# Differential attention in chunks of 384 queries, in five batches of 4, 4, 4, 3 and 3 key tiles

## The reference, cut to what matters

```python
Q, K, V = proj(q_w), proj(k_w), proj(v_w)      # (2, 8 heads, 2304 tokens, 64)
Q1, Q2 = Q[..., :32], Q[..., 32:]
K1, K2 = K[..., :32], K[..., 32:]
attn1 = softmax(Q1 @ K1^T * 32 ** -0.5)        # (2, 8, 2304, 2304)
attn2 = softmax(Q2 @ K2^T * 32 ** -0.5)
out = (attn1 - lam * attn2) @ V                # lam: one number per head
```

## Time and profile before

| what | value |
|---|---|
| time, median of 3 runs | 5568.89 us (5566.74 to 5574.1) |
| the profiled execution's own time | 5571.24 us |
| its span | 5569.4 us, 60834 instructions |
| PE, DVE, ACT, POOL busy over the span | 92%, 60%, 43%, 54% |
| differential attention: first pair to last normalised output | 245 to 3249 us |
| batch loop of it, first score to last value product's end | 282 to 3231 us |

### The profile page before, as it was taken

How to read it: one execution, slowest core, us unless ns; L and a number is a source line. 1 busy time by engine, 2 the same in 40 slices (tenths; PEclk the granted TensorE clock), 3 DMA queues, 4 the chain that set the end, 5 groups by cost and what they waited for, 6 DMA issues and landing times. The chain is left out here.

```text
span 5569.4 us, 60834 instructions
## 1 busy us (share of the span) xinstructions
PE 5106.0 (92%) x21620; PEld 2895.0 (52%) x21620; DVE 3339.3 (60%) x3947; ACT 2405.3 (43%) x4669; POOL 2985.2 (54%) x1379
## 2 busy tenths in 40 slices
PE   8799999999999999999999969879997898898699
PEld 4455545554555455545554424467774555555355
DVE  3466676677777767777677625465553445445484
ACT  3255555555555555555555522124442333333332
POOL 0088888888888888888888831046663000000000
PEclk9799999999999999999999978889998999999999
DMA  6611111111111111111111036442201000000101
GB/s 224 195 34 31 38 37 38 31 39 37 41 28 39 37 41 28 39 37 44 25 39 37 14 99 172 154 116 69 69 18 63 9 20 23 17 23 11 47 9 52
DMA packets 220119, 295.43 MB, mean 53 GB/s; under 512 B 77918, under 2 KB 186822, under 8 KB 212302
## 3 DMA queue, kind: packets, MB, share of 16 engines
q1 hardware_dynamic: 219856, 292.05, 18.6%
HBM read 178.11 MB, written 113.87 MB: 52 GB/s over the span
## 5 line engine op out<-in xcount | busy, mean ns | idle before, releaser
L658 POOL TENSOR_TENSOR diff_run_pool<-diff_run_pool,diff_probs 128x1024 f32<-128x1024 f32 (+1 forms) x960 | 2214.3, 2307 | 156.6 <-ACT diff_probs L505 19.6
L584 DVE TENSOR_REDUCE diff_maxes<-diff_max 128x1 f32<-128x768 f32 x1728 | 1539.2, 951 | 834.6 <-PE diff_max L425 833.4
L505 ACT ACTIVATE diff_probs<-diff_ring 128x512 f32<-128x512 f32 (+1 forms) x2880 | 1434.6, 558 | 1008.0 <-PE diff_ring L412 1002.2
L451 PE MATMUL diff_out_ps<-diff_probs,diff_vs 128*64 128x512 f32 (+1 forms) x5760 | 1222.4, 559 | 0.0
L425 PE MATMUL diff_max<-diff_ks,diff_qs 96*128 96x384 f32 x3456 | 977.0, 366 | 129.6 <-DVE diff_maxes L584 94.3
L412 PE MATMUL diff_ring<-diff_qs,diff_ks 97*128 97x512 f32 (+1 forms) x2880 | 1043.9, 397 | 3.3 <-ACT diff_probs L505 2.0
L425 PEld LDWEIGHTS diff_max<-diff_ks,diff_qs 96*128 96x128 f32 x3456 | 584.9, 191 | 472.9 <-DVE diff_maxes L584 392.6
L412 PEld LDWEIGHTS diff_ring<-diff_qs,diff_ks 97*128 97x128 f32 x2880 | 504.2, 188 | 388.0 <-issue 346.4
L451 PEld LDWEIGHTS diff_out_ps<-diff_probs,diff_vs 128*64 128x64 f32 x5760 | 371.8, 137 | 583.7 <-issue 441.7
L2041 POOL MEMSET ffn_before<- 128x128 f32 x1 | 0.2, 204 | 987.7 <-POOLq L63 987.7
L1373 POOL TENSOR_TENSOR causal_run_sum<-causal_run_sum,causal_probs 128x768 f32<-128x768 f32 (+2 forms) x208 | 340.7, 1638 | 74.7 <-ACT causal_probs L1247 52.7
(11 more groups left out here) (229 smaller groups left out, 5827.5 us busy)
## 6 DMA issues: line engine op xcount, KB each, us to landing
qk_hi<-proj_hi SPq DMA_DIRECT2D x12, 1536.0 KB, 5.8
qk_lo<-proj_lo SPq DMA_DIRECT2D x12, 1536.0 KB, 9.5
diff_qs<-qk_hi SPq DMA_DIRECT2D x64, 288.0 KB, 4.4
diff_ks<-qk_hi SPq DMA_DIRECT2D x64, 288.0 KB, 6.1
diff_recip<-row_factors SPq DMA_DIRECT2D x128, 128.0 KB, 2.8
o_rows<-diff_normed SPq DMA_DIRECT2D x64, 256.0 KB, 2.0
v_rows<-proj_vst SPq DMA_DIRECT2D x12, 768.0 KB, 7.6
diff_qs<-qk_lo SPq DMA_DIRECT2D x32, 288.0 KB, 5.3
```

Of the source, the lines that this page charges most:

```text
L451: mm = pe.matmul(out_ps[VD * j:VD * (j + 1), 0:w], vs[n % 2][:, g, j, :], probs[g % PBUF][:, j, 0:w], start=g == 0, stop=g == STEPS - 1, t ...
L505: act.activation(probs[g % PBUF][:, j, 0:w], ring[at % BANKS][:, 0:w], ACT.Exp, scale=SCALE).then_inc(s_taken, 1)
L584: dve.tensor_reduce(maxes[q % 2][:, j, s:s + 1, h], max_ps[u % 2][:, :, 0:T], AX.XY, ALU.max).then_inc(s_red, 1)
L658: pool.tensor_tensor(run_pool[:, :, 0:w], acc[:, :, 0:w], probs[g % PBUF][:, :, 0:w], ALU.add).then_inc(s_accp, 1)
```

## The change

All chunks are 384 queries wide, so a head has six. A chunk's 18 key tiles go in five batches of 4, 4, 4, 3 and 3 (`SIZES`). There are twelve buffers of probabilities of two times 384 columns, which is as many bytes as nine of two times 512, and a tile's buffer follows its number over all chunks (`tile % PBUF`) and no longer its number in the chunk. A step makes as many pairs as it makes scores' tiles, 18 to a chunk, and a pair stands ahead of each tile's two scores rather than behind single scores. 25 pairs are made before the loop instead of 32, and 18 of them before the first rows instead of 12. `ROWS_AT` and `NORMAL_AT` are batch 3 instead of 4; DVE's sums come after batches 1, 2 and 4 instead of 1, 3 and 5.

```diff
-    WIDE = 512
-    WIDTHS = (256, WIDE, WIDE, WIDE, WIDE)
-    PER_HEAD = len(WIDTHS)
+    WIDE = T
+    PER_HEAD = NC
...
-    BATCH = 3
-    BATCHES = STEPS // BATCH
+    SIZES = (4, 4, 4, 3, 3)
+    BATCHES = len(SIZES)
     BANKS = 3
-    PBUF = 9
+    PBUF = 12
...
-    SUMS_AT, ROWS_AT, COMPACT_AT, NORMAL_AT = 1, 4, 2, 4
+    SUMS_AT, ROWS_AT, COMPACT_AT, NORMAL_AT = 1, 3, 2, 3
...
-    add_after = {1: 1, 3: 2, 5: 3}
+    add_after = {1: 1, 2: 2, 4: 3}
...
-    LEAD = 2 * THIRDS * (WIDE // P) + 2 * (WIDE // P)
-    FIRST_PAIRS = 2 * THIRDS * (WIDTHS[0] // P)
+    FIRST_PAIRS = 2 * THIRDS * SUB
+    LEAD = 2 * FIRST_PAIRS - sum(SIZES[1:ROWS_AT + 1])
     pair_from = [LEAD]
     for e in range(TOTAL):
-        pair_from.append(min(pair_from[-1] + span(e // BATCHES)[1] // P, len(pairs)))
+        pair_from.append(min(pair_from[-1] + SIZES[(e + 1) % BATCHES], len(pairs)))
...
                     if e + 1 < TOTAL:
-                        for i in range(2 * BATCH):
-                            score(BATCH * (e + 1) + i // 2, i % 2)
-                            if i > 0 and us:
+                        for tile in tiles(e + 1):
+                            if us:
                                 max_pair(us.pop(0))
+                            for j in range(2):
+                                score(tile, j)
...
-                        act.wait_ge(s_pv, (tile - PBUF) // BATCH + 1)
+                        act.wait_ge(s_pv, batch_of(tile - PBUF) + 1)
```

More of the change, by code:

```diff
@@ L262, in differential_attention, with tiles, batch_of @@
     ND, NPOOL = len(on_dve) - 1, len(on_pool)
-    add_after = {1: 1, 3: 2, 5: 3}
+    add_after = {1: 1, 2: 2, 4: 3}
     TOTAL = CHUNKS * BATCHES
+    def tiles(e):
+        q, b = divmod(e, BATCHES)
+        return range(q * STEPS + sum(SIZES[:b]), q * STEPS + sum(SIZES[:b + 1]))
+    def batch_of(tile):
+        q, g = divmod(tile, STEPS)
+        return next(e for e in range(q * BATCHES, (q + 1) * BATCHES) if tile in tiles(e))
     def span(q):
-        c = q % PER_HEAD
-        return sum(WIDTHS[:c]), WIDTHS[c]
+        return q % PER_HEAD * T, T
     def queries(q):
@@ L287, in differential_attention @@
         if e + 1 < TOTAL:
-            for i in range(BATCH):
+            for tile in tiles(e + 1):
                 for j in range(2):
-                    slot["score", BATCH * (e + 1) + i, j] = len(slot)
+                    slot["score", tile, j] = len(slot)
         q, b = divmod(e, BATCHES)
@@ L446, in pv_batch @@
                             pe.wait_ge(s_oev, q)
-                    for tile in range(BATCH * e, BATCH * e + BATCH):
+                    for tile in tiles(e):
                         g = tile % STEPS
@@ L451, in pv_batch @@
                             mm = pe.matmul(out_ps[VD * j:VD * (j + 1), 0:w], vs[n % 2][:, g, j, :],
-                                           probs[g % PBUF][:, j, 0:w], start=g == 0, stop=g == STEPS - 1,
+                                           probs[tile % PBUF][:, j, 0:w], start=g == 0, stop=g == STEPS - 1,
                                            tile_position=(0, VD * j))
@@ L504, in exps @@
                         act.wait_ge(s_ring, at + 1)
-                        act.activation(probs[g % PBUF][:, j, 0:w], ring[at % BANKS][:, 0:w], ACT.Exp,
+                        act.activation(probs[tile % PBUF][:, j, 0:w], ring[at % BANKS][:, 0:w], ACT.Exp,
                                        scale=SCALE).then_inc(s_taken, 1)
@@ L534, in _ @@
                     if e + 1 < TOTAL:
-                        for i in range(BATCH):
-                            exps(BATCH * (e + 1) + i)
+                        for tile in tiles(e + 1):
+                            exps(tile)
                     if b == ROWS_AT and 0 <= q < CHUNKS - 1:
@@ L604, in add_up @@
                         dve.wait_ge(s_accp, q * NPOOL)
-                    acc = probs[on_dve[0] % PBUF] if i == 1 else run_dve
+                    acc = probs[(q * STEPS + on_dve[0]) % PBUF] if i == 1 else run_dve
                     to = sum_dve if i == ND else run_dve
-                    dve.tensor_tensor(to[:, :, 0:w], acc[:, :, 0:w], probs[g % PBUF][:, :, 0:w], ALU.add
+                    dve.tensor_tensor(to[:, :, 0:w], acc[:, :, 0:w], probs[(q * STEPS + g) % PBUF][:, :, 0:w], ALU.add
                                       ).then_inc(s_accd, 1)
@@ L656, in _ @@
                             pool.wait_ge(s_accp, q * NPOOL + i - 1)
-                        acc = probs[on_pool[0] % PBUF] if i == 1 else run_pool
-                        pool.tensor_tensor(run_pool[:, :, 0:w], acc[:, :, 0:w], probs[g % PBUF][:, :, 0:w], ALU.add
+                        acc = probs[(q * STEPS + on_pool[0]) % PBUF] if i == 1 else run_pool
+                        pool.tensor_tensor(run_pool[:, :, 0:w], acc[:, :, 0:w], probs[(q * STEPS + g) % PBUF][:, :, 0:w], ALU.add
                                            ).then_inc(s_accp, 1)
```

## The result

The changed kernel takes 5531.84 us (median of 4 runs, 5522.2 to 5548.05), where the kernel before took 5570.44 beside it: ratio 0.9934, interval 0.9905 to 0.9962, 38.6 us less. In a later comparison it took 5522.48 us (0.9911, 0.9896 to 0.9926). The forecast was 5485, 85 us less. The direction is right and the range holds the time, but less than half of the gain came. The profiled execution is the slowest of the four, 5548.05 us; where that matters a second trace of the same kernel, of 5519.92 us, stands beside it.

The account below looks back on a forecast made before the run. DVE's reductions set ordinary steps, ACT those without pairs, POOL close behind. Start 274.3, 96 chunks of 29.4 + 0.3, scaling 27.0 and end 1.5 gave 3154.0, 83.5 us earlier: 5485 us, range 5425 to 5560.

Parts of the forecast that it names:

- the walk of the chunk: Step times of one new chunk added up: 29.4 us, plus 0.3 us booked for DVE's waits.
- The start of the loop: Fewer pairs made before the loop: it starts at 274.3 us instead of 281.5.
- the first parts: Step's start until its value products: 3.41 us with four tiles, 2.61 with three, 0.9 more with the rows.
- ACT as the last in a step of four tiles: In a four-tile step's first part ACT's exponentials end last, 0.1 us behind DVE's reductions.
- No gain: Rival: DVE's reductions still set four-tile steps at 3.77 us; chunk 30.5 us, 5562 us; chance 0.14 with what lies near.
- the collision in every chunk: Rival: DVE's second sum and normalising each wait 1.83 us for POOL; chunk 32.3 us, 5735 us; chance 0.11.
- the first rival: POOL or PE at its best: DVE's waits fall into idle time, scaling costs nothing; chunk 29.4 us, 5430 us; chance 0.20.
- PE's walk: PE's first parts, value products, rows and sums over a chunk's five steps: 29.4 us.
- DVE's queue: DVE's waits for POOL and late factors delay step 4's first reduction: 0.3 us per chunk, bounds 0 and 2.9.
- In a head's last chunk: Scaling of values in step 2 delays step 3's reductions, pairs and scores: 1.8 us, fifteen times, 27.0 us.
- the sum: All terms added: POOL's last sum at 3154.0 us instead of 3237.5, 83.5 us earlier, so 5485 us.
- Its wait for DVE's sum: POOL's waiting for DVE's sum at chunk ends, 246.1 us before, falls under 100 us in total.

Follow-up runs that it names:

- filling the pause: Changed kernel with one score matmul of each head's last chunk made eight times over while DVE scales: 5505.66 us, ratio 0.9886 to the kernel before.
- scaling and normalising are moved: Changed kernel with the values' scaling in step 0 of a head's last chunk and normalising in step 4: 5466.71 us, ratio 0.981 to the kernel before.
- Two kernels of different tiling: Kernel before with each pair ahead of its tile's scores, 5462.92 us; changed kernel with scaling in step 0 and normalising in step 4, 5466.71 us.
- scaling early: Changed kernel with the values' scaling moved from step 2 to step 0 of a head's last chunk: 5482.64 us, ratio 0.9839 to the kernel before.
- both edits: Changed kernel with the scaling in step 0 of a head's last chunk and the reciprocal ahead of DVE's second sum: 5499.55 us, ratio 0.9874.
- six batches: Changed kernel with six batches of three key tiles, rows and normalising in batch 4, sums after 1, 3 and 5: 5506.49 us, ratio 0.9878.

## Why the prediction was wrong

The forecast time failed, by its size; the sign held, and so did the walk of the chunk, to 0.3 us.

*Right.* The start of the loop (0.8 us off in the profiled run), the first parts to 0.1 us, and ACT as the last in a step of four tiles. No gain (30.5 us a chunk) did not occur, nor the collision in every chunk (32.3), nor the first rival's 29.4 us.

*Right by luck.* The 29.70 us of an ordinary chunk. The forecast adds 29.4 for PE's walk and 0.3 for DVE's queue. In an ordinary chunk DVE's queue costs nothing, as the first rival has it: normalising is over at 1530.07, and the next reduction waits for PE.

```profile
1528.84 1.23 DVE L631 TENSOR_TENSOR diff_normed<-diff_out,diff_recip 128x384 f32<-128x384 f32 x1 [1.53 <-DMA diff_recip<-row_factors]
1530.31 3.55 DVE L592 TENSOR_REDUCE diff_maxes<-diff_max 128x1 f32<-128x768 f32 x4 [0.24 <-PE diff_max L432]
```

The 0.3 is PE's, whose first parts of four tiles take 3.50 and not 3.41 us, three times a chunk, and the one with the rows 3.60 and not 3.51. Two errors cancel.

*The step that failed* is "In a head's last chunk ... 1.2 to 2.3 us, I take 1.8 us, fifteen times". The slip is right, 1.6 us, as filling the pause showed. But the pause that it leaves PE costs a second time, through the clock, which the sum put at nothing: 55.6 us in all instead of 27.0. The sum took every duration at 2.4 GHz, because the stage before shows a mean of 1.00, and never asked what a pause of PE would do to that. The trace of the kernel before has the answer once, where DVE is late for the third pair: PE pauses for 0.93 us, and its next twelve value matmuls take 4.49 us instead of 2.79. The stretch behind the two rows has a granted clock of 0.50.

```profile
1853.21 0.61 PE L425 MATMUL diff_max<-diff_ks,diff_qs 96*128 96x384 f32 x2 [0.93 <-DVE diff_maxes L584]
1855.70 4.49 PE L451 MATMUL diff_out_ps<-diff_probs,diff_vs 128*64 128x512 f32 x12
...
1855.80:1859.20 3.40, 3.40 (x10) 0.95 (x12) 1.77 (x1) 0.86 (x2) 3.26 (x2) 0.50 0.36 107
```

*The second step that failed* is DVE's queue outside those chunks: "I book 0.3 us per chunk". From reciprocal to normalising it took the 5.01 us of one chunk at the stage's end for all, and a mean wait for POOL. Measured, the cost is nothing in an ordinary chunk and 1.6 us or more, with the pause and the clock behind it, in one where the factors come late and normalising meets a POOL sum. This was 30.4 us in the profiled run and 8.5 in the second trace, where 28.8 were booked (96 x 0.3), so two runs of one kernel differ by 22 us through it. With a step to spare it is 0. In the forecast's own terms, then, the miss of the profiled run is 28.6 us in the scaling, some 28 in PE's walk (0.3 in each chunk) and 1.6 in DVE's queue.

*POOL.* Its wait for DVE's sum was forecast under 100 us and is 185.6. Of this, 1.05 to 1.07 us stand in every ordinary chunk, 100 us in 95, since POOL's own work of a chunk is 28.6 us and not 29.2; the rest is the two excesses. It is 89.0 where scaling and normalising are moved.

*What the forecast never separated*: it priced the change as one thing. The order of PE's row alone gives the kernel before 111 us; the rest of the change, in the old order, costs 168; on top of the order it costs the 60 to 70 us by which the change stands behind. The row to see it in was there: PE idle for 100.4 of 2900 us, most of it waiting for DVE, as the waits of the kernel before from 300 to 3100 us say:

```profile
PE diff_max L425 <- DVE diff_maxes L584: 88.8, 359, 0.9
```

Two kernels of different tiling in which that idle time is gone, with PE busy for 99.7 and 99.8%, took 5463 and 5467 us, close to 5574 less 100.

*Left open.* What delays the small transfers in some chunks was not tried. It is not chance: counted from the first, chunks 2, 4, 16, 21, 24, 32, 35, 43, 63, 74 and 76 have more than 1.8 us from the factors' store to their load in each of the twelve traces with 96 chunks, whatever the batches. In the trace of scaling early, nine factors' stores are followed by their normalising more than 5.8 us after issue; an instruction load of 16 KB stands in the queues' rows between the two in seven of them, but also in 19 chunks that were not late.

## What to carry to other kernels

Read first what PE's idle time in the stage is worth, and who ends it: here one change of order took nearly all of it, and a new tiling added nothing to that. A wait that leaves PE idle is to be priced with the clock that may follow it, so work done once per head belongs in a step where its engine has time, and a result that comes back through DMAs wants a whole step to spare, not the latency of one chunk. When two edits come together, price each of them alone.

## What the runs showed of the hardware

A PE pause of 1.4 us in a stream that was otherwise full brought the granted clock from 1.00 to stretches of 0.63, mostly the 1.2 GHz level, and in the next stretch it was 1.00 again. Of the pauses over 1 us in the batch loop, 22 of 23 were followed by such a fall in the profiled run and 16 of 17 in the second trace (the stretch from 628 us stayed at 1.00), but with both edits only 5 of 12, of 1.1 to 1.4 us. None of the fourteen pauses of 0.7 us in the run of six batches was, while the one of 0.93 us in the kernel before was. Matmuls that do nothing useful, put into the pause, kept the fall away. What decides between pauses of the same length is not shown. The Trainium skill (TensorE: Matmul & The Clock Gate, section A second HAM failure mode: psum-queue depth-cycling) describes frequent small idle times between groups of matmuls that make the clock fall and rise again, at a price in throughput. These traces agree on the fall and the price, with 3.73 us for matmuls that take 2.16, and show them after single pauses.

A normalising on DVE that met a POOL sum begun 0.20 us earlier lasted 2.05 us, and 0.56 us where it met the end of one.

The latency of a chain of small DMAs is not a constant: from store to load it took 1.40 to 1.44 us in 65 of the 96 chunks of the profiled run and 1.49 to 2.75 in the others.
